# First dispatch units placed in the attention block's drain, weight split in smaller pieces, expert-output stores on SyncE

## What is computed

```python
def attention(q, k, v, wq, wk, wv, wo_w, wo_b):    # 16 heads of 16, banded: |i - j| <= 64
    qp, kp, vp = rope(q @ wq.T), rope(k @ wk.T), v @ wv.T
    scores = einsum(qp, kp) * sqrt(16)             # masked outside the band
    return softmax(scores) @ vp @ wo_w.T + wo_b

def experts(x, w_router, w_fc, w_gate, w_proj):    # E = 16, K = 2, cap = 16 rows per sequence and expert
    probs, ei = top_k(softmax(x @ w_router), 2)
    buf = zeros(E, cap, C)                         # per sequence: the first 16 tokens of each expert
    buf = buf.at[ei, pos].set(x, mode="drop")
    h = silu(buf @ w_gate) * (buf @ w_fc)          # 256 -> 128
    o = h @ w_proj                                 # 128 -> 256
    return sum_k probs_k * o[ei_k, pos_k]

x = x + tanh(g_xattn) * attention(layernorm(x), ctx, ctx, ...)
x = x + tanh(g_ffn)   * experts(layernorm(x), ...)
```

## Time and profile before

| | us |
|---|---|
| median of 3 runs | 1663.25 (1663.19 to 1664.76) |
| the profiled execution's own time | 1666.03 |
| its span, first to last instruction | 1664.2 |
| mean granted TensorE clock | 0.965 of full |

### The profile page before, as it was taken

One profiled execution on the slowest core, in us unless ns is written; L12 is line 12 of the kernel. 1 busy time (PEld: TensorE's weight loads), 2 busy tenths in 40 slices (PEclk: granted clock), 3 DMA queues, 4 the chain that ended last, 5 costly groups with the idle time before them and its releaser, 6 DMA issues. The chain is left out here.

```text
span 1664.2 us, 50836 instructions
## 1 busy us (share of the span) xinstructions
PE 1465.3 (88%) x16928; PEld 1198.7 (72%) x16928; DVE 1409.7 (85%) x3262; ACT 1158.7 (70%) x2289; POOL 970.6 (58%) x1478
## 2 busy tenths in 40 slices
PE   3899999999999999999999999999739999999990
PEld 3677677676767667676767767677429999999990
DVE  3688988988888898888889888888857899999973
ACT  3677777777777777777777777777626777767750
POOL 3566566566566656666665666566320566666666
PEclk9999999999999999999999999999858999999995
DMA  3124512211221121122112112211013899999987
GB/s 102 52 90 122 166 65 66 93 63 63 78 80 63 63 95 63 63 76 82 63 63 94 64 63 73 85 63 59 33 48 116 284 321 317 322 314 315 322 280 216
DMA packets 137543, 210.47 MB, mean 126 GB/s; under 512 B 16624, under 2 KB 69872, under 8 KB 137456
## 3 DMA queue, kind: packets, MB, share of 16 engines
q1 hardware_dynamic: 106736, 142.29, 26.5%
q0 software_dynamic: 12288, 33.57, 6.6%
q10 hardware_dynamic: 18432, 33.56, 5.5%
HBM read 125.47 MB, written 83.89 MB: 126 GB/s over the span
## 5 line engine op out<-in xcount | busy, mean ns | idle before, releaser
L596 DVE TRANSPOSE_TENSOR_REDUCE part_max<-ST 128x16 f32<-128x512 f32 x512 | 320.9, 683 | 35.1 <-PE ST L843 31.3
L425 ACT ACTIVATE probs_t<-ST 128x512 f32<-128x512 f32 x512 | 264.3, 603 | 32.1 <-PE ST L858 32.1
L870 PE MATMUL PO<-probs_t,v_aug 128*32 128x128 f32 x4096 | 194.0, 285 | 67.6 <-ACT probs_t L425 47.5
L870 PEld LDWEIGHTS PO<-probs_t,v_aug 128*32 128x32 f32 x4096 | 89.6, 109 | 160.0 <-ACT probs_t L425 142.6
L1203 POOL DMA_INDIRECT first<-eo_d,code x128 | 125.5, 980 | 133.1 <-DMA eo_d<-eo 78.5
L336 POOL TENSOR_TENSOR k_rot<-k_cos,k_sin 128x256 f32<-128x256 f32 x64 | 47.0, 734 | 244.5 <-DVE k_sin L634 244.5
L466 ACT ACTIVATE at_hi<-F 128x512 fp32r<-128x512 f32 x64 | 38.2, 597 | 189.9 <-PE F L890 189.9
L1326 PE MATMUL GU<-we_hi,s_hi 128*128 128x256 f32 x512 | 155.3, 303 | 0.0
L1203 POOL DMA_INDIRECT second<-eo_d,code x128 | 122.6, 958 | 42.4 <-issue 31.7
L1327 PE MATMUL GU<-we_hi,s_lo 128*128 128x256 f32 x512 | 144.9, 283 | 0.0
L1328 PE MATMUL GU<-we_lo,s_hi 128*128 128x256 f32 x512 | 144.9, 283 | 0.0
(11 more groups left out here) (155 smaller groups left out, 5510.9 us busy)
## 6 DMA issues: line engine op xcount, KB each, us to landing
eo_d<-eo ACTq DMA_DIRECT2D x128, 256.0 KB, 3.9
x_in_sb<-x SPq DMA_DIRECT2D x64, 256.0 KB, 2.8
c_in_sb<-ctx_t SPq DMA_DIRECT2D x64, 256.0 KB, 2.9
xr_sb<-x SPq DMA_DIRECT2D x64, 256.0 KB, 4.1
x_d<-x SPq DMA_DIRECT2D x64, 256.0 KB, 4.2
xn_d<-xn SPq DMA_DIRECT2D x64, 256.0 KB, 4.3
raw<-xn_d SPq DMA_DIRECT2D x64, 256.0 KB, 4.4
xr<-x_d SPq DMA_DIRECT2D x64, 256.0 KB
```

Of the source, the lines that this page charges most:

```text
L425: act.activation(probs_t[:, b, i].rearrange("p j q -> p (j q)"), ST[i][:], ACT.Exp) \
L596: dve.tensor_reduce(part_max[:, i, 0], ST[i][:].rearrange("p (c l) -> p c l", l=32), AX_X, ALU.max, apply_transpose=True).then_inc(M["part ...
L870: last = pe.matmul(PO[32 * j:32 * j + 32, i * SEQ:(i + 1) * SEQ], v_aug[:, n.par, b, head], probs_t[:, b, i, j], start=True, stop=True)
```

## The change

Units -14 to -2 of the expert stage are taken out of the expert block, which now starts at unit -1. They run inside the attention block, on SP, ACT, DVE and PE (POOL has no work in them): behind step 63 units -14 to -12, behind 64 units -11 to -8, behind 65 units -7 and -6, behind 66 units -5 and -4, behind 67 units -3 and -2. These load the xn2 of sequences 0 to 13, make `x_hi`, `x_lo` and `pick` for 0 to 9, and dispatch 0 to 7; the description of the change speaks of sixteen sequences. SP waits, before unit -14, for the last values product of the attention (`pv_done` at 512), since the constant `iota`, `pick` and `x_hi` now lie over attention buffers. DS is, in the attention block, the first two score banks.

The weights' chunks are split at other places: heads 0, then 1 to 3 in step 63, 4 and 5, 6 and 7, 8 and 9 in step 64, 10 and 11 in step 65; rests 0, then 1 to 3 in step 63, 4, then 5 and 6, then 7 in step 64, and 8, 9, 10, 11 singly in steps 66 to 69.

The `eo` stores are issued from SP, as the first thing of a unit, behind the `out_done` wait of the unit before. The diff follows, cut, in this order: what all engines run, SP's `dispatch`, ACT's and DVE's `step` of the attention block, the expert stage's stores (added on SP, taken from ACT), and the expert block's first unit. The bodies of the expert steps are the old ones, moved into functions `sp_step`, `act_step` and so on, which both blocks call.

```diff
+    early = {PAIRS - 1: (-14, -13, -12), PAIRS: (-11, -10, -9, -8), PAIRS + 1: (-7, -6), PAIRS + 2: (-5, -4),
+             PAIRS + 3: (-3, -2)}
-    def run(eng, step):
+    def run(eng, step, dispatch):
...
         for c in range(PAIRS - 4, PAIRS + 9):
             step(Pair(0, c))
+            for u in early.get(c, ()):
+                dispatch(u)
...
+        def dispatch(u):
+            if u == -14:
+                sp.wait_ge(M["rest_done"], 16)
+                sp.wait_ge(M["pv_done"], SEQS * 4)
+                for q in xn2_out:
+                    sp.wait_ge(q, 16 * 8)
+            X["sp"](sp, unit_at(u), on_at(u))
...
         def step(s): 
             if (s - 1).real:
                 copy_out_t(s - 1, 1)
+            if s.beyond == 0:
+                weight_heads(4, 6)
...
-            if s.beyond == -1:
-                weight_heads(0, 3)
             if (s - 1).real:
                 attention_head(s - 1)
+            if s.beyond == 0:
+                weight_heads(6, 8)
             if s.real:
                 for i in range(4):
                     exp_unit(s, 0, i)
+            if s.beyond == -1:
+                weight_heads(0, 1)
+            if s.real:
                 copy_out_t(s, 0)
-            if s.beyond == 0:
-                weight_heads(8, 10)
...
             if s.beyond == -1:
-                weight_heads(3, 8)
+                weight_heads(1, 4)
             if s.beyond == 0:
+                weight_heads(8, 10)
+            if s.beyond == 1:
                 weight_heads(10, CH)
...
         def step(s): 
...
             if (s - 1).real:
                 normalise(s - 1, 1)
+            if s.beyond == 0:
+                weight_rests(4, 5)
             if s.real:
                 shift_of(s, 0)
-            if s.beyond == -1:
-                weight_rests(0, 3)
...
             if s.beyond == 0:
-                weight_rests(7, 8)
+                weight_rests(5, 7)
             route_early(s)
+            if s.beyond == -1:
+                weight_rests(0, 1)
...
             if s.beyond == -1:
-                weight_rests(3, 7)
+                weight_rests(1, 4)
             if s.beyond == 0:
-                weight_rests(8, CH)
+                weight_rests(7, 8)
+            if s.beyond is not None and s.beyond > 1 and s.beyond < 6:
+                weight_rests(s.beyond + 6, s.beyond + 7)
...
+    def sp_step(sp, unit, on):
+        n = unit(OUTPUT)
+        if on(OUTPUT):
+            sp.wait_ge(M["eo_copied"], n.n + 1)
+            sp.dma_start(D["eo_d"][n.group][:, n.j * 2:n.j * 2 + 2], eo[n.turn(3)][:]) \
+                .then_inc(eo_out[n.turn(3)], 16)
+        n = unit(FETCH)
...
-            n = unit(OUTPUT)
-            if on(OUTPUT):
-                act.wait_ge(M["eo_copied"], n.n + 1)
-                act.dma_start(D["eo_d"][n.group][:, n.j * 2:n.j * 2 + 2], eo[:, n.turn(3)]) \
-                    .then_inc(eo_out[n.turn(3)], 16)
...
-        for u in range(FIRST, head):
+        for u in range(-1, head):
```

More of the change, by code:

```diff
@@ L1122, in expert_block @@
     iota_in = sem("iota_in")
[L1123 to L1135, removed]
-        for u in range(FIRST, head):
[L1137 to L1147, removed]
+    DS, HT, EO, GU = [], [], [], []
     def flat(a):
@@ L1160, in tokens @@
     def tokens(buf, n):
[L1162 to L1205, removed]
-                        in_offset=bass.IndirectOffsetOnAxis(ap=collect_row[:, k, n.n:n.n + 1], axis=0)) \
-                        .then_inc(rows_in[n.turn(3)], 16)
-        run_flat(pool, step)
@@ new lines, in pool_step @@
+    def pool_step(pool, unit, on):
+        n = unit(FETCH)
+        if on(FETCH):
+            pool.wait_ge(M["collect_done"], 1)
+            for r, q in enumerate(eo_out):
+                pool.wait_ge(q, len(range(r, (n.group + 1) * GROUP, 3)) * 16)
+            wait_for(pool, M["out_done"], n.n - 2)
+            for k, dst in ((0, first), (1, second)):
+                pool.indirect_dma_start(
+                    out=dst[:, n.turn(3)], out_offset=None,
+                    in_=D["eo_d"][n.group].rearrange("r e c -> (r e) c"),
+                    in_offset=bass.IndirectOffsetOnAxis(ap=collect_row[:, k, n.n:n.n + 1], axis=0)) \
+                    .then_inc(rows_in[n.turn(3)], 16)
@@ L1319, in _ @@
-        run_flat(dve, step)
-    @block.tensor
-    def _(pe):
+        if unit(GATE).n == 0:
+            rows_and_weights()
+        n = unit(HIDDEN)
+        if on(HIDDEN):
+            dve.wait_ge(M["h_hi_done"], n.n + 1)
+            wait_for(dve, M["eo_done"], n.n - 1)
+            dve.tensor_tensor(flat(h_lo[:, n.slot(2)]), HT[n.slot(2)][:, 0:2 * P],
+                              flat(h_hi[:, n.slot(2)]).bitcast(F32), ALU.subtract).then_inc(M["h_lo_done"], 1)
+        n = unit(REST)
+        if on(REST) and n.n % 2 == 0:
+            dve.wait_ge(M["x_hi_done"], n.n // 2 + 1)
+            wait_for(dve, M["ds_done"], n.n - 2)
+            dve.tensor_tensor(flat(two(x_lo, n, 4)), flat(two(x_in_sb, n, 4)), flat(two(x_hi, n, 4)).bitcast(F32),
+                              ALU.subtract).then_inc(M["x_lo_done"], 1)
@@ new lines, in dve_step @@
+        n = unit(GATE)
+        if on(GATE):
+            gu = GU[n.slot(2)][:].rearrange("p (e f n) -> p e f n", e=2, f=2)
+            dve.wait_ge(M["gate_done"], n.n + 1)
+            dve.tensor_tensor(gate[n.slot(2)][:], gate[n.slot(2)][:], gu[:, :, 1], ALU.mult).then_inc(M["hid_done"], 1)
+        n = unit(COLLECT)
+        if on(COLLECT):
+            dve.wait_ge(rows_in[n.turn(3)], n.landed(3, 32))
+            dve.wait_ge(x1_in[n.n // 2 % 3], pair_landed(n, 3))
+            dve.scalar_tensor_tensor(out=xr[:, n.turn(6)], in0=first[:, n.turn(3)],
+                                     scalar=weight[:, 0, bass.ds(n.n, 1)], in1=xr[:, n.turn(6)],
+                                     op0=ALU.mult, op1=ALU.add).then_inc(M["y_part_done"], 1)
@@ new lines, in dve_step @@
+        n = unit(DISPATCH)
+        if on(DISPATCH):
+            dve.wait_ge(M["s_hi_done"], n.n + 1)
+            dve.tensor_tensor(tokens(s_lo, n), DS[n.slot(2)][:].rearrange("p (k e s) -> p (k e) s", k=KC, s=CAP),
+                              tokens(s_hi, n).bitcast(F32), ALU.subtract).then_inc(M["s_lo_done"], 1)
+        n = unit(COLLECT)
+        if on(COLLECT):
+            dve.wait_ge(M["y_part_done"], n.n + 1)
+            dve.scalar_tensor_tensor(out=xr[:, n.turn(6)], in0=second[:, n.turn(3)],
+                                     scalar=weight[:, 1, bass.ds(n.n, 1)], in1=xr[:, n.turn(6)],
+                                     op0=ALU.mult, op1=ALU.add).then_inc(M["out_done"], 1)
@@ L1375, in _ @@
-        run(pe, step)
+        n = unit(OUTPUT)
+        if on(OUTPUT):
+            for done in ("h_hi_done", "h_lo_done"):
+                pe.wait_ge(M[done], n.n + 1)
+            wait_for(pe, M["eo_copied"], n.n - 1)
+            for e in range(2):
+                at = n.j * (2 * DIM) + e * DIM
+                last = split_matmul(EO[n.slot(2)][:, e * DIM:(e + 1) * DIM],
+                                    [h[:, n.slot(2), e] for h in (h_hi, h_lo)],
+                                    [w[:, at:at + DIM] for w in w_down])
+            last.then_inc(M["eo_done"], 1)
@@ new lines, in pe_step @@
+        n = unit(DISPATCH)
+        if on(DISPATCH):
+            for done in ("pick_done", "x_hi_done", "x_lo_done"):
+                pe.wait_ge(M[done], n.pair + 1)
+            wait_for(pe, M["s_lo_done"], n.n - 1)
+            slot = n.slot(4)
+            for k in range(KC):
+                out = DS[n.slot(2)][:, k * SLOTS:(k + 1) * SLOTS]
+                pe.matmul(out, x_hi[:, slot, k * P:(k + 1) * P], pick[:, slot], start=True, stop=False)
+                last = pe.matmul(out, x_lo[:, slot, k * P:(k + 1) * P], pick[:, slot],
+                                 start=False, stop=True)
+            last.then_inc(M["ds_done"], 1)
```

323 lines of the change are left out of this document (164 added, 159 removed).

## The result

| | before | changed |
|---|---|---|
| median, us | 1664.01 (4 runs, 1663.19 to 1667.4) | 1650.49 (4 runs, 1649.35 to 1653.34) |
| ratio | | 0.9918 [0.9898, 0.9937] |
| profiled execution, us | 1666.03 | 1650.61 |
| span, us | 1664.2 | 1648.8 |
| granted clock | 0.965 | 0.971 |

The change makes the kernel 0.82% faster: 13.5 us where 8.3 were forecast, and 1650.49 lies just under the range of 1651 to 1661.5. The direction was right, the size was not. (The 1663.25 us from which the prediction starts is the median of three of the four runs of the kernel before.)

The account below looks back on a forecast made before the run. PE was taken to pace the steady units, chains the drain and block change, POOL the end. -18.4 (block change) + 9.7 (drain) + 0.4 (left over) = -8.3 us, from the median 1663.25 to 1655.0; range 1651 to 1661.5.

Parts of the forecast that it names:

- Part 1: Weight pieces at new places in steps 63 and 64: step 64 runs 3.2 us earlier.
- Part 2: Dispatch behind step 64: second layernorm of pair 63 at 1220.0, 2.9 us earlier, and its logits copy at 1224.9.
- Part 3: Rest of the drain, DVE's stream filling up: attention block ends at 1245.4, 9.7 us later than before.
- rival B: Dispatch hardly overlaps in the drain, each sequence a PE, ACT, DVE round trip: 1659.4 to 1662 us; chance 0.15.
- the 1.3 us of it in the range: Allowance in the drain, twice 0.65 us, for POOL's routing operations waiting beside DVE's rests; not added to the sum.
- Part 4: Block change: 18.4 us of loads and dispatches go, 0.4 us is left; unit -1 at 1245.8, 8.3 us earlier.
- Part 5: The eo stores issued from SP in the expert units: counted 0, bounds -2 (PE's idle) and +2 us.
- rival C: Steady units gain too, through ACT's relief and POOL's smaller backlog: 2 to 4 us more; chance 0.12.
- Rival D: The eo stores land late in SP's queue, stalling ACT, then PE: 1675.6 us if units grow 0.2 us; chance 0.07.

Follow-up runs that it names:

- Experiment 1: The kernel before with only the eo stores moved from ACT to SP: 1659.09 us, 0.9966 of the kernel before.
- Experiment 3: The changed kernel with the eo stores put back on ACT: 1656.19 us, 0.9947 of the kernel before.

## Why the prediction was right and wrong

**Part 1 (step 64 3.2 us earlier): right.** Pair 63's statistics are at 1212.56 for 1218.10; of these 5.5 us 1.9 were there at pair 60, and 3.65 remain. `ranked` is at 1199.76, PE waits 3.50 us for it still.

**Part 2 (normed2 at 1220.0, logits copy at 1224.9): right.** They are at 1218.05 and 1222.88, 1.95 and 2.0 before the forecast, which is what the execution was ahead from its start. ACT's `s_hi` of sequence 1 is what the second layernorm waits behind, as said.

**Part 3 (last `place` at 1245.4): right to 1 us.** It ends at 1242.55, or 1244.4 with the 1.9 us put back. DVE does not pause from 1225.3 to 1241 and sets the end: rival B's round trips are not there. POOL's operations beside a rest took 1.23 us for 0.32, at 1233.05 and 1239.55. That is what the Trainium skill (SBUF — State Buffer, "Who interferes with whom") says of a GpSimd read beside such a DVE operation, and this trace agrees; but PE and DVE had work in the meantime (DVE's next step at 1240.81 did not wait), so the 1.3 us of it in the range were not used, and 1655 rather than 1656.5 was the right term.

**Part 4 (block change 18.4 us shorter, 0.4 left): right.** First matmul 0.62 us after the last `place` ends. Unit -1 comes 9.05 us earlier net of the head start, for 8.3. The clock rises 2.8 us into unbroken work (1245.95), not 4.0.

**Part 5 (the store, counted 0): the step that failed.** The prediction saw the 21.7 us that DVE waits for the gate, and then said "PE is full, so at most its 2.06 us of idle can be won". The bound was wrong, not the mechanism, which rival C had. Idle time in the stretches is what the records leave uncovered, and with records of 0.28 us every 0.12 a stall of less than about 0.16 us is covered. Experiment 1 measures the term at -5.7 us (-7.7 to -3.7), outside the -2 to +2 allowed. With it the sum is -8.3 - 5.7 = -14.0, 1649.3, and the interval of the ratio holds it (0.9898 to 0.9937 of 1663.25 is 1646.3 to 1652.8). Rival C had 2 to 4 us and a chance of 0.12; with the bound gone it should have been the forecast. Of its two roads the runs show the first, DVE freed from the gate; the other, POOL's backlog at the end, shrank by 0.4 us only (77.69 to 77.29).

**Rival D (one queue for everything): not seen** in the 1664 us condition. SP issues the `eo` store behind the `out` store, 0.36 us after the copy has ended, and 4.1 us pass to its landing where it was 3.9:

```profile
1421.11 0.34 SPq L1192 DMA_DIRECT2D out<-xr  x1
1421.49 0.46 SPq L1171 DMA_DIRECT2D eo_d<-eo  x1
1422.09 0.37 SPq L1186 DMA_DIRECT2D raw<-xn_d  x1
```

By the rule of the Trainium skill (DMA: Bandwidth & Descriptors, "Queues, rings and completion order"), that a DMA engine goes round between the queues that have work, the store loses a turn of its own. 0.2 us is all that these traces show of that, far from the 7 us at which it would decide.

**What was luck.** 1.55 us of the span's difference had come by pair 6, before any edited step. That it cancels in the medians is not shown: in the 1664 us condition the traces with the old attention block reach that point at 104.6 to 105.1 us, those with the new one at 101.9, 102.4, 103.0 and 104.9. Experiment 3, the one at 104.9, has no such head start and still measures -8.8, so parts 1 to 4 were off by 0.5 us, with an interval of some 2 us to either side.

## What to carry to other kernels

"The bound engine is full" has to be read from the pace of its units or the number of its instructions in a stretch, held against the best unit of the same stage (2.82 us here, 2.89 the mean), not from its idle time, because overlapping records hide short stalls. The median and the mean of that spacing say different things: an edit of the ordinary unit shows in the one, a few long units in the other. A wait for one's own last operation, with the DMA issue behind it, in the middle of a unit of an engine that works in order cost 4 to 6 us here; at the unit's end, or on another engine, it did not, but in the 1738 us condition both moves lost time, so measure in the condition that counts. Where a drain hangs on one engine, its filler work belongs in the waits ahead of the full stretch; of 4.8 us moved there, 4.5 came off the end.

## What was unexpected of the hardware

- Matmuls of 128x256 are recorded 0.28 us long at a distance of 0.12 us, at full clock.
- The same program has two conditions: the kernel before takes 1664 or 1738 us, the changed kernel moves 319 or 254 GB/s in the expert stage, and an edit can be faster in the one (0.9971) and slower in the other (1.0035, 1.0062).
- The clock went up 4.0 us into unbroken work at the block change before, 2.8 us after. In the start-up the same operation came up to 3.2 us apart in different executions, with a granted clock of 0.77 to 0.89 from 30 to 60 us.
- POOL's `same_as`, 0.32 us alone, took 1.23 to 1.30 us three times in the changed kernel (1202.1, 1233.1 and 1239.5 us), each time beside a DVE rest with two inputs from SBUF.
